# Router logits with stationary router weights, and the transposed expert choice behind the first gate turn

## What is computed

```python
# layer 0: 8 experts, the best 2      (flat = layernorm(x), 512 x 768)
scores = sqrt(softplus(flat @ gate_w))                       # gate_w 768 x 8
_, indices = top_k(scores + gate_bias, 2)
weights = take(scores, indices); weights /= weights.sum()
out = shared(flat) + sum_e combine[:, e] * expert_e(flat)    # silu(x @ W1) * (x @ W3) @ W2
# layer 2: 3 experts, the best 2
probs = sigmoid(x @ router_w + bias)                         # router_w 768 x 3
# layer 3: 8 experts, the best 1, 64 places for each expert
probs = softmax(x @ router_w)                                # router_w 768 x 8
```

## Time and profile before

| | |
|---|---|
| time, median of 3 runs | 3494.69 us (3494.08 to 3500.54) |
| the profiled execution, its own time | 3493.54 us |
| its span in the profile | 3491.7 us |
| mean granted TensorE clock, share of full | 0.93 |
| busy: PE, DVE, ACT, POOL | 90%, 50%, 22%, 41% |

### The profile page before, as it was taken

One profiled execution on the slowest core, in us unless ns is written; L12 is line 12 of the kernel. 1 busy time (PEld: TensorE's weight loads), 2 busy tenths in 40 slices (PEclk: granted clock), 3 DMA queues, 4 the chain that ended last, 5 costly groups with the idle time before them and its releaser, 6 DMA issues.

```text
span 3491.7 us, 39990 instructions
## 1 busy us (share of the span) xinstructions
PE 3152.6 (90%) x14323; PEld 2503.3 (72%) x14333; DVE 1743.6 (50%) x2942; ACT 751.3 (22%) x1316; POOL 1421.5 (41%) x1007
## 2 busy tenths in 40 slices
PE   8999798999999968989767879899999998979978
PEld 3576577788888846768546568678888886758868
DVE  7635797565554363347675245533334436551131
ACT  1044111332323211122123121210111103121122
POOL 1121386353345423645300024346666664426500
PEclk9999898999999978999877779989999999989977
DMA  2010365121122201212200222123233322213213
GB/s 77 24 49 28 122 215 160 50 77 59 55 68 77 73 27 51 86 57 87 64 0 9 65 85 77 54 61 100 89 100 94 95 86 77 68 32 103 81 44 112
DMA packets 91264, 256.93 MB, mean 74 GB/s; under 512 B 10335, under 2 KB 10975, under 8 KB 90852
## 3 DMA queue, kind: packets, MB, share of 16 engines
q1 hardware_dynamic: 80352, 219.45, 21.0%
q10 hardware_dynamic: 10788, 35.83, 3.0%
HBM read 253.67 MB, written 1.57 MB: 73 GB/s over the span
## 4 chain that ended last, share of the span: by engine, by line
PE 83%; DVE 11%; issue 3%; ACT 2%; POOL 1%; DMA 0%; DVEq 0%; ACTq 0%; POOLq 0%
PE ps L413 21%; PE ps L417 21%; PE ps L418 21%; PE ps L880 2%; DVE aux L1811 2%; PE ps L515 1%; PE ps L509 1%; PE ps L1117 1%; PE ps L988 1%; PE ps L1019 1%; PE ps L768 1%; PE ps L779 1%; PE ps L761 1%; PE ps L753 1%; DVE hot L2130 1%
## 5 line engine op out<-in xcount | busy, mean ns | idle before, releaser
L361 POOL TENSOR_SCALAR w_hi<-raw 128x768 fp32r<-128x768 f32 x498 | 455.6, 915 | 1836.3 <-PE ps L413 1493.5
L364 POOL TENSOR_TENSOR w_lo<-raw,w_hi 128x768 fp32r<-128x768 f32 x498 | 974.2, 1956 | 41.5
L413 PE MATMUL ps<-H_hi,w_hi 128*128 128x512 f32 x804 | 319.1, 397 | 20.3 <-issue 15.5
L417 PE MATMUL ps<-H_lo,w_hi 128*128 128x512 f32 x804 | 316.7, 394 | 0.0
L418 PE MATMUL ps<-H_hi,w_lo 128*128 128x512 f32 x804 | 316.3, 393 | 0.0
L413 PE MATMUL ps<-B_hi,w_hi 128*128 128x512 f32 x720 | 291.7, 405 | 21.0 <-DVE B_lo L1609 14.9
L413 PE MATMUL ps<-A_hi,w_hi 128*128 128x512 f32 x780 | 308.2, 395 | 0.0
L417 PE MATMUL ps<-A_lo,w_hi 128*128 128x512 f32 x780 | 304.9, 391 | 0.0
L418 PE MATMUL ps<-A_hi,w_lo 128*128 128x512 f32 x780 | 304.0, 390 | 0.0
L417 PE MATMUL ps<-B_lo,w_hi 128*128 128x512 f32 x720 | 283.3, 393 | 0.0
L418 PE MATMUL ps<-B_hi,w_lo 128*128 128x512 f32 x720 | 282.8, 393 | 0.0
(11 more groups left out here) (435 smaller groups left out, 6068.0 us busy)
## 6 DMA issues: line engine op xcount, KB each, us to landing
raw<-stream_dram SPq DMA_DIRECT2D x558, 384.0 KB, 3.1
w_ring<-w_dram ACTq DMA_DIRECT2D x39, 384.0 KB, 3.6
u_rows<-rows_dram ACTq DMA_DIRECT2D x8, 768.0 KB, 6.5
rows<-rows_dram ACTq DMA_DIRECT2D x7, 768.0 KB, 4.0
w_last<-w_dram ACTq DMA_DIRECT2D x9, 384.0 KB, 3.7
x<-x_dram ACTq DMA_DIRECT2D x1, 1536.0 KB, 9.1
out_dram<-x ACTq DMA_DIRECT2D x1, 1536.0 KB, 5.1
orf<-orf_dram ACTq DMA_DIRECT2D x6, 192.0 KB, 3.0
```

Source lines behind the costliest of these rows:

```text
L361: pool.tensor_scalar(w_hi[:, b // 3, b % 3], raw[:, b // 3, b % 3], 1.0, 1.0, ALU.mult, ALU.mult)\
L364: pool.tensor_tensor(w_lo[:, b // 3, b % 3], raw[:, b // 3, b % 3], w_hi[:, b // 3, b % 3], ALU.subtract)\
L413: mm = pe.matmul(o, wh, xh, start=first, stop=False, skip_group_check=True)
L417: pe.matmul(o, wh, xl, start=False, stop=False, skip_group_check=True)
```

## The change

The logits are computed with the operands exchanged: `router_t` makes the router's 8 (or 3) columns stationary and lets all 512 tokens of A move, 6 x 3 = 18 matmuls in place of 72. The result has experts on the partitions, so DVE copies it to `row`, PE transposes it in four pieces into bank 7, and DVE copies that to `gate_s` as before. The first expert step is taken out of the loop, and `combine_rows` is put behind its gate turn. In layer 2 the router has 3 columns in place of 4.

```diff
@@ -808,17 +808,19 @@
-            def router_n(X, c0, n):
+            def router_t(X, c0, n):
 
                 use(6)
-                for m in range(NT):
-                    for k in range(KC):
-                        if m == 0:
-                            pe.wait_ge(dve_to_pe, normed[k])
-                        c = slice(m * P, m * P + P)
-                        mm = mm3(ps[:, 6, m * 8:m * 8 + n], X[0][:, k, c], X[1][:, k, c], small_hi[:, k, c0:c0 + n],
-                                 small_lo[:, k, c0:c0 + n], k == 0, k == KC - 1)
+                for k in range(KC):
+                    pe.wait_ge(dve_to_pe, normed[k])
+                    mm = mm3(ps[0:n, 6], small_hi[:, k, c0:c0 + n], small_lo[:, k, c0:c0 + n], X[0][:, k], X[1][:, k],
+                             k == 0, k == KC - 1)
                 done(mm, 6, "dve")
+                use(7)
+                pe.wait_ge(dve_to_pe, S.due(dve_to_pe))
+                for m in range(NT):
+                    mm = pe.transpose(ps[:, 7, m * 8:m * 8 + n], row[0:n, m * P:m * P + P], ident[0:n, 0:n])
+                done(mm, 7, "dve")
@@ -828,8 +830,11 @@
             def experts(X, what, n, per_chunk):
-                with S.loop(what, n) as i:
+
+                def expert(first):
                     turn_t(X, "act", normed, last=False)
+                    if first:
+                        combine_rows()
                     pe.wait_ge(dve_to_pe, S.due(dve_to_pe))
@@ -845,6 +850,10 @@
                     turn_t(H, "dve", chunks_due())
+
+                expert(True)
+                with S.loop(what, n - 1):
+                    expert(False)
@@ -940,8 +949,7 @@
                 norm_of(x)
-                router_n(A, R0, 8)
-                combine_rows()
+                router_t(A, R0, 8)
                 experts(A, "experts0", 2, True)
@@ -1055,8 +1063,7 @@
                 norm_of(x)
-                router_n(A, R2, 4)
-                combine_rows()
+                router_t(A, R2, 3)
                 experts(A, "experts2", 8, False)
@@ -1072,7 +1079,7 @@
                 norm_of(x)
-                router_n(A, R3, 8)
+                router_t(A, R3, 8)
                 to_nodes(acc)
@@ -2099,7 +2106,10 @@
             def router_logits(n):
                 dve.wait_ge(tile_for["dve"], S.due(tile_for["dve"]))
-                freed(dve.tensor_copy(gate_s[:, 0, :, 0:n], ps[:, 6, 0:32].rearrange("p (m e) -> p m e", m=NT)[:, :, 0:n]), 6)
+                freed(dve.tensor_copy(row[0:n, :], ps[0:n, 6]), 6)
+                mark(dve_to_pe)
+                dve.wait_ge(tile_for["dve"], S.due(tile_for["dve"]))
+                freed(dve.tensor_copy(gate_s[:, 0, :, 0:n], ps[:, 7, 0:32].rearrange("p (m e) -> p m e", m=NT)[:, :, 0:n]), 7)
```

More of the change, by code:

```diff
@@ L809, in gelu_mlp @@
                     turn_t(H, "dve", chunks_due(), staged=True)
-            def router_n(X, c0, n):
+            def router_t(X, c0, n):
                 use(6)
-                for m in range(NT):
-                    for k in range(KC):
-                        if m == 0:
-                            pe.wait_ge(dve_to_pe, normed[k])
-                        c = slice(m * P, m * P + P)
-                        mm = mm3(ps[:, 6, m * 8:m * 8 + n], X[0][:, k, c], X[1][:, k, c], small_hi[:, k, c0:c0 + n],
-                                 small_lo[:, k, c0:c0 + n], k == 0, k == KC - 1)
-                done(mm, 6, "dve")
+                for k in range(KC):
+                    pe.wait_ge(dve_to_pe, normed[k])
+                    mm = mm3(ps[0:n, 6], small_hi[:, k, c0:c0 + n], small_lo[:, k, c0:c0 + n], X[0][:, k], X[1][:, k],
+                             k == 0, k == KC - 1)
+                done(mm, 6, "dve")
+                use(7)
+                pe.wait_ge(dve_to_pe, S.due(dve_to_pe))
+                for m in range(NT):
+                    mm = pe.transpose(ps[:, 7, m * 8:m * 8 + n], row[0:n, m * P:m * P + P], ident[0:n, 0:n])
+                done(mm, 7, "dve")
             def combine_rows():
```

## The result

The changed kernel takes 3456.4 us (median of 4 runs, 3452.86 to 3456.45); the kernel before, 3497.4 us over its 4 runs. The ratio is 0.9882, with a 95% interval of 0.9869 to 0.9894: about 41 us faster. Forecast were 3455 us and 40.3 us less; the range was 3449 to 3467. The profiled execution went from 3493.54 to 3452.86 us, its span from 3491.7 to 3451.1.

The account below looks back on a forecast made before the run. PE, busy 90% of the span, was taken as the bound. 18.8 + 15.3 + 9.3 + 2.2 - 5.3 = 40.3 us off 3493.54 gives 3453.2; plus 1.15 for the median, rounded to 3455; range 3449 to 3467.

Parts of the forecast that it names:

- The router's matmuls: Routers of layers 0, 2, 3: 18 matmuls replace 72 pairs, clock rises after 5 us, last result at F + 6.70.
- F: Start of the first router matmul in a layer; each step is counted from it, and it does not move.
- Rival A: Router stays at half clock to its end; gate turns start at it, losing about 2 us each; 3462 us, chance 0.25.
- The transposition: Behind the router: DVE copies to row, then four PE transposes from F + 7.57, 0.77 us; gate turn at F + 8.34.
- The choice hidden: Layers 0 and 2: PE's wait for comb_n, 8.59 and some 5 us, moves beside the gate turn, at least 24 us.
- The pause behind the gate turn: Behind the first gate turn PE transposes comb_n and waits for sel_now: 2.8 us in layer 0, 2.5 in layer 2.
- the forecast's added 0.4: Layers 0 and 2, pause behind the gate turn: us added to sel_now's copy because POOL will be splitting; 0.9 and 0.62.
- Rival B: Pause behind gate turns brings half clock stretches and slower copies, 5.4 us lost; 3460 us, chance 0.14 alone or in part.
- Layer 3: Only the router counts: gate_s copied at F + 8.63 in place of F + 17.95, 9.3 us gained.
- Rivals C and D: C: router matmuls run several passes, near 3531 us, chance 0.03. D: gate turn waits for something else, nothing gained, 0.01.

Follow-up runs that it names:

- e9: The change with one 128 x 512 reciprocal on DVE between the copy to row and the memset that signals PE, in all three layers; 3471.4 us.
- e5: The change with two 128 x 512 reciprocals added to DVE's choice chain in layers 0 and 2; 3457.1 us.
- e6: The kernel before with only the operands exchanged, choice still ahead of the expert loop, plus two 128 x 512 reciprocals in the choice chain; 3485.1 us.
- e8: The change with one 128 x 256 reciprocal on DVE ahead of the copy to comb_t, lengthening the pause behind the first gate turn; 3459.3 us.
- e7: The change with all remaining columns of small_hi stationary: 32, 24 and 20 in place of 8, 3 and 8; 3459.8 us.
- e2: The kernel before, 72-matmul router kept, with only the first expert step written out and combine_rows behind its gate turn; 3484.8 us.

## Why the prediction held

*The router's matmuls.* Forecast F + 6.70 for the last result, measured F + 6.78. The open question was whether the clock would rise with them. It rose 5.4 and 5.5 us after F in layers 0 and 2 of the first trace, and 4.3 us after it in layer 3; I had taken 5. The 2.9 us that I gave for dense work after idle runs from the transposes at 2286.1; the first gate matmul starts at 2286.81, 2.3 us ahead of the rise. Rival A thus fell in its first half, and e9 priced its second.

*The transposition.* Forecast start F + 7.57, measured F + 7.83: the copy took 0.68 as the 16-row copy did, but started 0.11 after the matmul in place of 0.04, and memset and pick-up took 0.26 in place of 0.15. The four transposes took 0.31 in place of 0.77, for I had priced them by rows at the half clock. The two errors cancel to 0.2 us: the gate turn started at F + 8.14, forecast F + 8.34. The clock did not fall in the 1.05 us of idle. The Trainium skill's remark (TensorE: Matmul & The Clock Gate, Part 4: PE-mode transpose) that transposes don't count as busy cost nothing here; the window after them shows 1.00. e9 shows that a pause of 4.4 us does let it fall.

*The choice hidden.* This held; e5 and e6 show it directly.

*The pause behind the gate turn.* From the last gate matmul to the next useful one 2.60 us in layer 0 and 2.27 in layer 2, less one step of 0.23: 2.4 and 2.0, against 2.8 and 2.5. The term that was oversized is the transposes' 0.9 us and DVE's start behind them: together 0.94 forecast, 0.64 measured, again priced by rows at the half clock. sel_now took 0.76 in layer 0 and 0.44 in layer 2, against 0.9 and 0.62. Both copies started while POOL was subtracting. The Trainium skill's rule (SBUF — State Buffer, Who interferes with whom), that a DVE copy in its two-port mode and a GpSimd instruction exclude each other and the one issued later is blocked until the other is over, agrees with these rows: POOL's instructions end at 1345.76 and 2280.99, 0.35 and 0.36 us after the copies' starts, and the copies took 0.21 and 0.22 us more than with POOL idle (0.55 and 0.22). The small copy of layer 2 ended 0.08 us after POOL's instruction. e8, made for another question, is the counter-test: its longer pause puts both copies behind POOL's work, and they take as long as with POOL idle.

```profile
1350.03 0.55 DVE L2062 COPY sel_now<-sel 16x768 f32 x1 [0.24 <-DVE comb_t L2129]
...
2290.50 0.21 DVE L2063 COPY sel_now<-sel 16x128 f32 x1 [0.23 <-DVE comb_t L2129]
```

The waits were short because the copy came when POOL was near its end. Nothing in the forecast says that it would, though all three traces of the change have the same 0.35 us; the forecast's added 0.4 was twice too much.

*Rival B* came true in half: a half clock stretch behind layer 2's pause in all three traces of the change, 1.6 us. The sum had left it out. By layer, forecast and measured: 17.1 and 17.5; 13.9 and 13.0; 9.3 and 10.2. Layer 2 is short by rival B's 1.6 us, less the shorter tail and the earlier gate turn. Layer 3 is over by 0.9, mostly since gate_s was copied at F + 7.85, not F + 8.63: the transposes started 0.14 us earlier, as the router ended at F + 6.38 there, and from their start to the copy it took 0.42 us, not 1.06 (their price again). The rest of its stretch moved with it.

*Rivals C and D.* In the three traces of the change no router matmul took more than 0.43 us from start to start, and no matmul of the gate turns in layers 0 and 2 had idle time before it.

So the mechanism held, and that 40.3 came within 0.4 us of 40.7 is partly luck: the pauses were priced 0.9 us too high together, the gate turns' starts 0.4 too late, layer 3's gain 0.9 too small, some 2 us in all, and the half clock stretch that the sum left out took 1.6 back.

What stays open: why the half clock followed the 1.4 us pause of layer 2 in all three traces of the change and the 1.8 us pause of layer 0 in none, though in e7 it came in both. The length of the pause doesn't decide it: e2 and e9 have the same two pauses (1.8 and 1.5 us), later after F, and the clock stayed at 1.00 behind all four. Nor does what follows: in layer 2 PE comes back to two matmuls of 16 rows (L841, 1.12 us) before its next weight block, which would make it the longer break in dense work, 3.3 us against 2.6; but e2 and e9 have these too, and e7's layer 0 hasn't. No run tells it.

## What to carry to other kernels

When a product has one narrow side, make that side the stationary one: 18 matmuls with 512 moving columns did the work of 72 pairs of load and matmul with 8, and a small transposition of the result paid for the layout. A chain of small vector instructions that only a later step needs belongs behind work of the matrix engine that doesn't need it, and the transposes that connect the two belong some matmuls ahead of the first wait, not at it. And two such edits need not add up: here each alone left the matrix engine slow at the next stage's start (5.1 and 4.8 us at the half clock), and only both together did not.

## What was not expected of the hardware

PE was busy without a pause for the last 12 us of the 72 matmuls with 8 moving columns and stayed at 1.2 GHz, and the dense turn that follows without a pause (e2) still started there and had 2.4 GHz only 4.8 us later. PE busy with 512 moving columns and only 8 stationary ones had 2.4 GHz after 5.4 us in layer 0, 4.3 in layer 3 and 3.2 in layer 2 of e8, and kept it over 1.05 us of idle and four transposes; an idle time of 4.4 us (e9) lost it. After such a loss the next dense turn ran 2.3 us (the kernel before) to 5.6 us (e9's layer 2) before the clock rose. A pause of 1.4 to 1.8 us behind a turn is sometimes followed by some 3.3 us at 1.2 GHz, at a cost of 1.6 us, about as much as the pause itself.
